# Softplus as one ScalarE function in place of Abs, Relu, Exp, Ln and a VectorE sum

## The chip, the cores and the metric

The kernel runs on one core of a Trainium2 chip. The metric is the device time of one execution in microseconds. A core has TensorE (PE, matmuls and transposes), VectorE (DVE), ScalarE (ACT), GpSimd (POOL) and SyncE (SP, which issues all DMAs here). Each engine runs its own instruction stream in order, and they wait for one another on semaphores.

## The reference

Four sequences of 512 steps pass through a selective state space mixer and a feed-forward part with routed low-rank additions, each followed by a layer norm. D = 2048 channels, N = 16 states, R = 64. Everything is float32.

```python
u, gate = jnp.split(hidden_states @ W_in.T, 2, axis=-1)
u = silu(causal_depthwise_conv(u, conv_w) + conv_b)
dt, Bm, Cm = jnp.split(u @ Wx.T, [R, R + N], axis=-1)      # each then through an rmsnorm
delta = jax.nn.softplus(dt @ Wdt.T + dt_bias)
# per step: state = exp(delta * A) * state + (delta * u) * B ;  y = sum over N of state * C
y = (y + u * D_param) * silu(gate)
x = layernorm(x + y @ W_out.T)
x = layernorm(x + x @ W.T + b + lora(x))
```

## The kernel before

Channels lie on the partitions: D is cut into 16 tiles of 128 channels, time (512) lies along the free axis. The mixer goes through 256 units (b, g, n): sequence b (4), group g of four channel tiles (4), state n (16). A unit is

- on SP a fetch of one row of B for all partitions,
- on POOL `drive` = du times that row (128x2048, L1202),
- on ACT four `decay` = exp(delta * A) (L1038) into three PSUM buffers in turn,
- on DVE four `scan` (L803), which write the states over drive,
- on PE sixteen transposes (`turn`, L674) into two banks `state_t`, which three DVE additions (`add`, L818) and, for the fourth, ACT (`scale`) and POOL (`sum`) weigh with C and add to `y_acc`.

Between the units the engines work off other jobs. Products with W_in and with the feed-forward weights (`u_mm`, `g_mm`, `f_mm`, L698 to L700) run as three passes of a high and a low part. W_out's product (`o_mm`, L721) uses plain float32. `w_high` on ACT (L1072) and `w_low` on POOL (L1228) split weights into these parts. `u_conv`, `u_silu`, `g_tanh` (L1087) and `g_silu` finish the products. At the end of a group `y_turn` on PE turns y back, `y_skip` on DVE (L879) adds D_param * u, and `y_gate` on POOL (L1224) multiplies with the gate. An `o_mm` of sequences 0 to 2 needs all 16 `y_gate` of its sequence. These products share three PSUM banks (`BANKS`), each held from its first matmul until its last reader.

delta is made by `delta_job` for half a group, two tiles, at a time, 32 halves in all. `delta_mm` on PE (L743, L744) makes a tile in a bank. `d_abs` is two ACT passes over it: Abs of x + dt_bias into `delta` (L1119), and Relu of the same back into the bank (L1120). `d_exp` makes exp(-|x|) in `delta` (L1125), `d_ln` makes ln(1 + that) (L1131). `d_sum` on DVE (L848) adds the bank to `delta`, which gives softplus, and gives the bank back. Then `du` on POOL (L1217) makes delta * u for the whole group, ahead of the group's drives, and the decays read delta. The delta of a group is made while the group before it is scanned. That of group 0 is made at the end of the sequence before, or, for sequence 0, before anything is scanned.

The order of every engine's instructions is not written by hand. `make_plan` puts down each piece with a due time and an assumed duration, what it needs and which bank or buffer it takes, and `arrange` walks through time and gives each engine the ready piece with the earliest due time. The instructions are then issued in that order, with waits on the semaphores of what they need. Exp and Ln lie in different function tables here, so that a table load (ACT_TABLE_LOAD), which the compiler places, stands between them.

## Time and profile before

| | |
|---|---|
| median of 3 runs | 2586.82 us (2584.71 to 2592.55) |
| the profiled execution | 2587.63 us, span 2585.8 us |
| TensorE busy | 2216.7 us, 86% |
| VectorE busy | 2191.0 us, 85% |
| GpSimd busy | 1797.8 us, 70% |
| ScalarE busy | 1426.0 us, 55% |
| mean clock granted to TensorE | 0.914 of full speed |

The span runs from the first instruction to the last. Busy time is the time in which an engine executes something, and an engine that is busy for most of the span can still not be the one that others wait for in a given stretch. The trace also says of each instruction how long its engine stood idle before it and which instruction ended that idle time.

### The profile page before, as it was taken

The page shows a single profiled execution, that of the slowest core. Times are in us where ns is not written, and L with a number is a line of the kernel's source. Part 1 is how long each engine was busy: PE and PEld are TensorE (multiplying, and loading weights), DVE is VectorE, ACT ScalarE, POOL GpSimd, SP SyncE. Part 2 cuts the span into 40 slices and gives each one's busy share as a digit, 9 for nine tenths or more (in the row PEclk, how much of TensorE's full clock was granted, in tenths as well). Part 3 has the DMA queues.
Part 4 walks back from the last instruction along what each step waited for, and adds up shares of the span by engine and source line. Part 5 has one row for each costly group of instructions (what it writes and reads, how often), then busy time and mean ns, then how long its engine had stood idle before and what let it go on. Part 6 is the DMA issues. An engine that isn't in the chain of part 4 may idle for free.

```text
span 2585.8 us, 30936 instructions
## 1 busy us (share of the span) xinstructions
PE 2216.7 (86%) x10528; PEld 1609.6 (62%) x10528; DVE 2191.0 (85%) x2681; ACT 1426.0 (55%) x2155; POOL 1797.8 (70%) x768
## 2 busy tenths in 40 slices
PE   6978779887789979899979979899979987888977
PEld 5756557676645557677855556677845556665545
DVE  3449889999969799899969989999978999999831
ACT  3357566664456475655556565655556566554421
POOL 3359989988667679767657866867658887678600
PEclk9988879999879989899979989999969998988988
DMA  4256555554222325755533324556523334343213
GB/s 157 62 187 220 187 184 181 179 188 159 83 76 84 98 90 185 255 179 188 168 101 91 107 86 128 182 191 191 162 79 97 107 92 139 108 162 96 78 49 114
DMA packets 152652, 353.53 MB, mean 137 GB/s; under 512 B 17776, under 2 KB 27376, under 8 KB 152496
## 3 DMA queue, kind: packets, MB, share of 16 engines
q1 hardware_dynamic: 152496, 351.56, 42.4%
q8 instruction: 84, 1.38, 0.2%
q14 instruction: 72, 0.59, 0.1%
HBM read 282.65 MB, written 68.85 MB: 136 GB/s over the span
## 4 chain that ended last, share of the span: by engine, by line
PE 53%; DVE 31%; issue 8%; ACT 4%; POOL 3%; DMA 1%; SPq 0%; DVEq 0%; POOLq 0%; ACTq 0%
PE bank L721 16%; DVE drive L803 14%; PE state_t L674 12%; DVE y_acc L818 7%; PE bank L698 6%; PE bank L700 6%; PE bank L699 6%; PE bank L674 3%; DVE scratch L825 2%; PE bank L756 2%; POOL drive L1202 1%; DVE ln_stats L898 1%; DVE channels L839 1%; PE bank L744 1%; DVE channels L879 1%
## 5 line engine op out<-in xcount | busy, mean ns | idle before, releaser
L1202 POOL TENSOR_TENSOR drive<-delta_u,b_bcast 128x2048 f32<-128x2048 f32 x256 | 1170.9, 4577 | 302.0 <-PE state_t L674 301.0
L803 DVE TENSOR_TENSOR_SCAN drive<-decay,drive 128x512 f32<-128x512 f32 x1024 | 1195.1, 1203 | 34.5 <-POOL drive L1202 30.9
L1038 ACT ACTIVATE decay<-delta,a_sb 128x512 f32<-128x512 f32 x1024 | 700.2, 689 | 474.6 <-DVE drive L803 468.3
L674 PE MATMUL state_t<-identity,drive 128*128 128x128 f32 x4096 | 630.9, 296 | 219.8 <-DVE drive L803 147.5
L674 PEld LDWEIGHTS state_t<-identity,drive 128*128 128x128 f32 x4096 | 510.5, 151 | 433.0 <-DVE drive L803 201.0
L698 PE MATMUL bank<-cols_high,w_split 128*128 128x512 f32 (+1 forms) x1312 | 564.7, 430 | 51.2 <-POOL w_split L1228 37.4
L818 DVE SCALAR_TENSOR_TENSOR y_acc<-state_t,c_rows,y_acc 128x512 f32<-128x512 f32 x720 | 513.8, 735 | 65.0 <-PE state_t L674 60.0
L700 PE MATMUL bank<-cols_high,w_split 128*128 128x512 f32 (+1 forms) x1312 | 528.6, 403 | 0.0
L699 PE MATMUL bank<-cols_low,w_split 128*128 128x512 f32 (+1 forms) x1312 | 527.1, 402 | 0.0
L721 PE MATMUL bank<-channels,w_raw 128*128 128x512 f32 x1024 | 487.3, 607 | 5.9 <-POOL channels L1224 5.3
L1208 POOL TENSOR_TENSOR y_acc<-y_acc,scaled 128x512 f32<-128x512 f32 x240 | 308.9, 1287 | 143.3 <-ACT scaled L1052 143.1
L698 PEld LDWEIGHTS bank<-cols_high,w_split 128*128 128x128 f32 (+1 forms) x1312 | 255.9, 195 | 104.5 <-issue 35.8
L700 PEld LDWEIGHTS bank<-cols_high,w_split 128*128 128x128 f32 (+1 forms) x1312 | 253.8, 193 | 59.8
L721 PEld LDWEIGHTS bank<-channels,w_raw 128*128 128x128 f32 x1024 | 183.2, 195 | 160.8 <-issue 159.7
L699 PEld LDWEIGHTS bank<-cols_low,w_split 128*128 128x128 f32 (+1 forms) x1312 | 256.0, 195 | 42.0
L1052 ACT ACTIVATE scaled<-state_t,c_rows 128x512 f32<-128x512 f32 x240 | 163.6, 682 | 184.5 <-PE state_t L674 150.5
L1228 POOL TENSOR_TENSOR w_split<-w_raw,w_split 128x512 fp32r<-128x512 f32 (+1 forms) x114 | 145.4, 1287 | 121.6 <-ACT w_split L1072 121.6
L825 DVE SCALAR_TENSOR_TENSOR scratch<-bank,conv_w_sb,scratch 128x511 f32<-128x511 f32 (+2 forms) x192 | 142.7, 743 | 46.7 <-ACT scratch L1078 42.2
L1224 POOL TENSOR_TENSOR channels<-channels,scratch 128x512 f32<-128x512 f32 x64 | 80.9, 1277 | 72.5 <-DVE channels L879 72.1
L889 DVE TENSOR_TENSOR rows<-bank,rows 128x512 f32<-128x512 f32 x80 | 54.2, 678 | 90.6 <-PE bank L674 90.2
L1072 ACT ACTIVATE w_split<-w_raw 128x512 fp32r<-128x512 f32 (+1 forms) x114 | 70.4, 620 | 41.6 <-PE bank L700 32.6
L1217 POOL TENSOR_TENSOR delta_u<-delta,channels 128x512 f32<-128x512 f32 x64 | 80.1, 1287 | 14.2 <-DVE delta L848 14.2
(100 smaller groups left out, 1474.6 us busy)
## 6 DMA issues: line engine op xcount, KB each, us to landing
w_split<-w_split SPq DMA_DIRECT2D x288, 512.0 KB, 3.6
b_bcast<-b_rows SPq DMA_DIRECT2D x256, 256.0 KB, 3.4
w_raw<-in_w_out SPq DMA_DIRECT2D x128, 256.0 KB, 2.9
w_raw<-in_w_in SPq DMA_DIRECT2D x96, 256.0 KB, 3.6
gates<-scratch SPq DMA_DIRECT2D x64, 256.0 KB, 2.5
scratch<-gates SPq DMA_DIRECT2D x64, 256.0 KB, 4.7
w_raw<-in_x_cols SPq DMA_DIRECT2D x32, 256.0 KB, 4.1
rows<-in_x_rows SPq DMA_DIRECT2D x4, 2048.0 KB, 9.2
```

Source lines behind the costliest of these rows:

```text
L674: last = engine.transpose(bank[0:tile.shape[1], i * P:(i + 1) * P], tile, identity[:, :])
L698: engine.matmul(bank[:, :], high[:, k % WK, :], cols_high[:, k, :], start=first, stop=False)
L699: engine.matmul(bank[:, :], high[:, k % WK, :], cols_low[:, k, :], start=False, stop=False)
L700: engine.matmul(bank[:, :], low[:, k % WK, :], cols_high[:, k, :], start=False, stop=last).then_inc(signal[stage])
L721: engine.matmul(bank[:, :], tile[:, k % WK, :], chan[s % 2][:, k, :], start=(k == tiles[0]), stop=(k == tiles[-1])).then_inc(signal["o_mm"])
L803: engine.tensor_tensor_scan(state, decay[(GT * s + t) % DECAYS][:, :], state, 0.0, ALU.mult, ALU.add).then_inc(signal["scan"])
L818: engine.scalar_tensor_tensor(y_acc[:, tt, :], bank[:, :], c, y_acc[:, tt, :], ALU.mult, ALU.add).then_inc(signal["add"])
L825: m = engine.scalar_tensor_tensor(conv[:, back:T], bank[:, 0:T - back], conv_w[:, j, KC - 1 - back:KC - back], conv[:, back:T], ALU.mult, ...
L1038: engine.activation(decay[i % DECAYS][:, :], delta[:, g % 2, t, :], ACT.Exp, scale=a_sb[:, j, n:n + 1]).then_inc(signal["decay"])
L1052: engine.activation(scaled[:, :] if n else y_acc[:, ADDED, :], bank[:, :], ACT.Copy, scale=c_rows[b % 2][:, ADDED, n:n + 1]).then_inc(sign ...
L1202: engine.tensor_tensor(drive[key % DRIVES][:, :, :], du[:, :, :], row, ALU.mult).then_inc(signal["drive"])
L1208: engine.tensor_tensor(total, total, scaled[:, :], ALU.add).then_inc(signal["sum"])
```

## The change

`d_abs`, `d_exp`, `d_ln` and `d_sum` become one piece `softplus` on ACT. For the two tiles of a half it runs ACT.Softplus with dt_bias as bias from the bank straight into `delta`, and gives both banks back. The plan assumes 3.8 us for a half. `du` and `decay` now wait for `softplus`. Softplus is in a function table of its own. Apart from that the planner's rules are the same, but since pieces and durations differ, it arrives at another order on all engines.

```diff
--- before.py
+++ after.py
@@ -251,11 +251,8 @@
             key = (b, g, t)
             put("PE", due, 0.46, "delta_mm", key, [there, ("dt_low", b), *old, *beside, *[("delta_mm", (b, g, t - 1))] * (t % 2)],
                 take=[("bank", ("delta_mm", (b, g, x))) for x in tiles] if t % 2 == 0 else [], give=[("dt", w)] if t % 2 else [])
-            put("ACT", due + 0.6, 1.18, "d_abs", key, [("delta_mm", key), *old])
-        put("ACT", due + 0.9, 1.1, "d_exp", (b, g, half), [("d_abs", (b, g, t)) for t in tiles])
-        put("ACT", due + 0.9, 3.7, "d_ln", (b, g, half), [("d_exp", (b, g, half))])
-        for t in tiles:
-            put("DVE", due + 1.2, 0.6, "d_sum", (b, g, t), [("d_ln", (b, g, half))], give=[("bank", ("delta_mm", (b, g, t)))])
+        put("ACT", due + 0.9, 3.8, "softplus", (b, g, half), [("delta_mm", (b, g, t)) for t in tiles] + old,
+            give=[("bank", ("delta_mm", (b, g, t))) for t in tiles])
 
     def y_job(b, g, t, due):
         key, last = (b, g, t), UNITS.index((b, g, N - 1))
@@ -392,7 +389,7 @@
         q = 4 * s
         put("SP", q - 10, 0.35, "fetch", s, [("b_store", b)] + ([("drive", s - 2)] if s > 1 else []), kb=256)
         if n == 0:
-            put("POOL", q - 8.5, 4.95, "du", (b, g), [("d_sum", (b, g, t)) for t in range(GT)] +
+            put("POOL", q - 8.5, 4.95, "du", (b, g), [("softplus", (b, g, half)) for half in range(2)] +
                 [("u_silu", (b, g * GT + t)) for t in range(GT)] + ([("drive", s - 1)] if s else []))
             for half in range(2 if g else 0):
                 delta_job(b, g, half, q - 4 * N + 16 * half + 8)
@@ -402,7 +399,7 @@
             [("turn", (s - DRIVES, tt)) for tt in range(TT)] if s >= DRIVES else [("lora_rest", 0)]))
         for t in range(GT):
             i = GT * s + t
-            put("ACT", i - DECAYS - 0.5, 0.605, "decay", (s, t), [("d_sum", (b, g, t))] + (
+            put("ACT", i - DECAYS - 0.5, 0.605, "decay", (s, t), [("softplus", (b, g, t // 2))] + (
                 [("scan", divmod(i - DECAYS, GT))] if i >= DECAYS else []))
             put("DVE", i, 1.13, "scan", (s, t), [("drive", s), ("decay", (s, t))])
         for tt in range(TT):
@@ -841,11 +838,6 @@
                     bank, gate = banks[place["bank", ("g_mm", key)]], scratch[place["scratch", ("g", key)]]
                     e.wait_ge(*done("g_tanh", key))
                     engine.scalar_tensor_tensor(gate[:, :], gate[:, :], 1.0, bank[:, :], ALU.add, ALU.mult).then_inc(signal["g_silu"])
-                elif stage == "d_sum":
-                    b, g, t = key
-                    dst = delta[:, g % 2, t, :]
-                    e.wait_ge(*done("d_ln", (b, g, t // 2)))
-                    engine.tensor_tensor(dst, banks[place["bank", ("delta_mm", key)]][:, :], dst, ALU.add).then_inc(signal["d_sum"])
                 elif stage == "dt_low":
                     e.wait_ge(*done("dt_cols", key))
                     if key:
@@ -1032,7 +1024,7 @@
                     s, t = key
                     b, g, n = UNITS[s]
                     j, i = g * GT + t, GT * s + t
-                    e.wait_ge(*done("d_sum", (b, g, t)))
+                    e.wait_ge(*done("softplus", (b, g, t // 2)))
                     if i >= DECAYS:
                         e.wait_ge(*done("scan", divmod(i - DECAYS, GT)))
                     engine.activation(decay[i % DECAYS][:, :], delta[:, g % 2, t, :], ACT.Exp, scale=a_sb[:, j, n:n + 1]).then_inc(signal["decay"])
@@ -1108,28 +1100,18 @@
                     e.wait_ge(*done("ssm_turn_b", key))
                     engine.activation(cols[0:N, :], banks[place["bank", ("ssm_turn_b", key)]][0:N, :], ACT.Copy,
                                       scale=b_ln_w[:, :]).then_inc(signal["b_cols"])
-                elif stage == "d_abs":
-                    b, g, t = key
-                    j, bank = g * GT + t, banks[place["bank", ("delta_mm", key)]]
-                    e.wait_ge(*done("delta_mm", key))
-                    if (b, g) >= (0, 2):
-                        b0, g0 = (b, g - 2) if g >= 2 else (b - 1, g + 2)
-                        e.wait_ge(*done("decay", (UNITS.index((b0, g0, N - 1)), t)))
-                        e.wait_ge(*done("du", (b0, g0)))
-                    engine.activation(delta[:, g % 2, t, :], bank[:, :], ACT.Abs, bias=dt_bias[:, j:j + 1])
-                    engine.activation(bank[:, :], bank[:, :], ACT.Relu, bias=dt_bias[:, j:j + 1]).then_inc(signal["d_abs"])
-                elif stage == "d_exp":
+                elif stage == "softplus":
                     b, g, half = key
                     for t in (2 * half, 2 * half + 1):
-                        e.wait_ge(*done("d_abs", (b, g, t)))
-                        m = engine.activation(delta[:, g % 2, t, :], delta[:, g % 2, t, :], ACT.Exp, scale=-1.0)
-                    m.then_inc(signal["d_exp"])
-                elif stage == "d_ln":
-                    b, g, half = key
-                    e.wait_ge(*done("d_exp", key))
-                    for t in (2 * half, 2 * half + 1):
-                        m = engine.activation(delta[:, g % 2, t, :], delta[:, g % 2, t, :], ACT.Ln, bias=1.0)
-                    m.then_inc(signal["d_ln"])
+                        j = g * GT + t
+                        e.wait_ge(*done("delta_mm", (b, g, t)))
+                        if (b, g) >= (0, 2):
+                            b0, g0 = (b, g - 2) if g >= 2 else (b - 1, g + 2)
+                            e.wait_ge(*done("decay", (UNITS.index((b0, g0, N - 1)), t)))
+                            e.wait_ge(*done("du", (b0, g0)))
+                        m = engine.activation(delta[:, g % 2, t, :], banks[place["bank", ("delta_mm", (b, g, t))]][:, :], ACT.Softplus,
+                                              bias=dt_bias[:, j:j + 1])
+                    m.then_inc(signal["softplus"])
                 elif stage in ("o_copy", "f_copy"):
                     s, h = key[:2]
                     cols = scratch_of((stage[0], key))
@@ -1212,7 +1194,7 @@
                         e.wait_ge(*done("drive", UNITS.index((b, g, 0)) - 1))
                     for t in range(GT):
                         j = g * GT + t
-                        e.wait_ge(*done("d_sum", (b, g, t)))
+                        e.wait_ge(*done("softplus", (b, g, t // 2)))
                         e.wait_ge(*done("u_silu", (b, j)))
                         m = engine.tensor_tensor(du[:, t, :], delta[:, g % 2, t, :], chan[b % 2][:, j, :], ALU.mult)
                     m.then_inc(signal["du"])
```

Lines of the changed kernel lie lower: its softplus is L1112, decay L1030, g_tanh L1079, w_high L1064, scan L800, drive L1184, w_low L1210, du L1199, y_gate L1206, turns L671, o_mm L718, delta_mm L740 and L741, products L695 to L697.

Three places of the order follow. The first is on ScalarE at the program's start, where the second half of group 0's delta is made; before, from the `w_high` of dt_slot on:

```order
L1072 ACTIVATE dt_slot<-w_raw 128x256
L1119 ACTIVATE delta<-bank,dt_bias_sb 128x512
L1120 ACTIVATE bank<-bank,dt_bias_sb 128x512
L1087 ACT_TABLE_LOAD
L1087 ACTIVATE scratch<-bank 128x512
L1125 ACTIVATE delta<-delta 128x512 x2
L1072 ACTIVATE w_split<-w_raw 128x512
L1131 ACT_TABLE_LOAD
L1131 ACTIVATE delta<-delta 128x512 x2
L1072 ACTIVATE w_split<-w_raw 128x512 x2
L1038 ACT_TABLE_LOAD
L1038 ACTIVATE decay<-delta,a_sb 128x512
```

and in the changed kernel, from the same instruction on:

```order
L1064 ACTIVATE dt_slot<-w_raw 128x256
L1112 ACT_TABLE_LOAD
L1112 ACTIVATE delta<-bank,dt_bias_sb 128x512 x2
L1079 ACT_TABLE_LOAD
L1079 ACTIVATE scratch<-bank 128x512
L1064 ACTIVATE w_split<-w_raw 128x512
L1030 ACTIVATE decay<-delta,a_sb 128x512
L1112 ACT_TABLE_LOAD
L1112 ACTIVATE delta<-bank,dt_bias_sb 128x512 x2
L1064 ACTIVATE w_split<-w_raw 128x512
L1030 ACT_TABLE_LOAD
```

The Abs and Relu passes around it are gone, and one load, two Softplus passes and one load stand where Exp, load, Ln and load stood. Before, the second half's passes begin only behind the last row shown; in the changed kernel its Softplus is the second L1112 pair, in the same rows.

The second is on GpSimd at the start of sequence 1. The four L1208 are the last additions to y_acc of sequence 0, L1224 is y_gate, L1217 du, L1202 drive. Before:

```order
L1208 TENSOR_TENSOR y_acc<-y_acc,scaled 128x512
L1202 TENSOR_TENSOR drive<-delta_u,b_bcast 128x2048
L1208 TENSOR_TENSOR y_acc<-y_acc,scaled 128x512 x4
L1224 TENSOR_TENSOR channels<-channels,scratch 128x512 x4
L1217 TENSOR_TENSOR delta_u<-delta,channels 128x512 x4
L1202 TENSOR_TENSOR drive<-delta_u,b_bcast 128x2048 x5
L1208 TENSOR_TENSOR y_acc<-y_acc,scaled 128x512
```

and in the changed kernel, where these are L1190, L1206, L1199 and L1184:

```order
L1190 TENSOR_TENSOR y_acc<-y_acc,scaled 128x512
L1184 TENSOR_TENSOR drive<-delta_u,b_bcast 128x2048
L1190 TENSOR_TENSOR y_acc<-y_acc,scaled 128x512 x4
L1206 TENSOR_TENSOR channels<-channels,scratch 128x512 x2
L1199 TENSOR_TENSOR delta_u<-delta,channels 128x512 x4
L1206 TENSOR_TENSOR channels<-channels,scratch 128x512
L1184 TENSOR_TENSOR drive<-delta_u,b_bcast 128x2048 x4
L1206 TENSOR_TENSOR channels<-channels,scratch 128x512
```

du has moved ahead of the last two y_gate, and the last y_gate behind four drives. At the starts of sequences 2 and 3 the last one stands behind two drives.

The third is on TensorE at the same place. Before, behind the first half's delta_mm, with the last turns of sequence 0, y_turn (from y_acc), the second half's delta_mm and then W_out's product:

```order
L674 MATMUL state_t<-identity,drive 128x128 x8
L674 MATMUL bank<-identity,y_acc 128x128 x16
L743 MATMUL bank<-dt_cols,dt_slot 128x512
L744 MATMUL bank<-cols_rest,dt_slot 128x512
L743 MATMUL bank<-dt_cols,dt_slot 128x512
L744 MATMUL bank<-cols_rest,dt_slot 128x512
L721 MATMUL bank<-channels,w_raw 128x512 x18
L674 MATMUL state_t<-identity,drive 128x128 x8
```

and in the changed kernel:

```order
L671 MATMUL state_t<-identity,drive 128x128 x8
L740 MATMUL bank<-dt_cols,dt_slot 128x512
L741 MATMUL bank<-cols_rest,dt_slot 128x512
L740 MATMUL bank<-dt_cols,dt_slot 128x512
L741 MATMUL bank<-cols_rest,dt_slot 128x512
L671 MATMUL bank<-identity,y_acc 128x128 x16
L695 MATMUL bank<-cols_high,w_split 128x512
L696 MATMUL bank<-cols_low,w_split 128x512
L697 MATMUL bank<-cols_high,w_split 128x512
```

Both halves' delta_mm now stand ahead of y_turn. Behind y_turn stand 48 matmuls of products (the last three rows, sixteen times over) where 18 of W_out's stood, and W_out's product begins behind these, another pair of delta_mm and 28 transposes of the new sequence's units.

## Rows read from the trace of the kernel before

**Rows 1.** The page: busy time, the chain by engine, and one group of matmuls.

```profile
PE 2216.7 (86%) x10528; PEld 1609.6 (62%) x10528; DVE 2191.0 (85%) x2681; ACT 1426.0 (55%) x2155; POOL 1797.8 (70%) x768
...
PE 53%; DVE 31%; issue 8%; ACT 4%; POOL 3%; DMA 1%; SPq 0%; DVEq 0%; POOLq 0%; ACTq 0%
...
L698 PE MATMUL bank<-cols_high,w_split 128*128 128x512 f32 (+1 forms) x1312 | 564.7, 430 | 51.2 <-POOL w_split L1228 37.4
```

**Rows 2.** Busy by stretches, two sums and one stretch; columns PE, PEld, DVE, ACT, POOL.

```profile
sum 1465.00, PE 1242.65 PEld 976.40 DVE 1400.07 ACT 842.26 POOL 1095.28; mean PE 310.66 PEld 244.10 DVE 350.02 ACT 210.56 POOL 273.82
...
sum 393.00, PE 383.50 PEld 215.26 DVE 371.66 ACT 234.94 POOL 315.20; mean PE 127.83 PEld 71.75 DVE 123.89 ACT 78.31 POOL 105.07
...
177.00:325.00 148.00, 117.83 (x577) 91.71 (x576) 131.80 (x144) 96.06 (x154) 142.51 (x67) 0.87 0.62 208
```

**Rows 3.** The same two sets of stretches, d_sum (L848) alone.

```profile
sum 1465.00, DVE 17.77; mean DVE 4.44
...
sum 393.00, DVE 7.62; mean DVE 2.54
```

**Rows 4.** ScalarE's groups of instructions by line: count, busy us, mean ns, idle before.

```profile
L1038 ACT ACTIVATE decay<-delta,a_sb 128x512 f32<-128x512 f32 x1024 | 700.2, 689 | 474.6 <-DVE drive L803 468.3 <-DVE delta L848 3.5
...
L1072 ACT ACTIVATE w_split<-w_raw 128x512 fp32r<-128x512 f32 (+1 forms) x114 | 70.4, 620 | 41.6 <-PE bank L700 32.6 <-issue 4.6 <-DMA w_raw<-in_w_in 4.0
L1078 ACT ACTIVATE scratch<-bank,conv_b_sb,conv_w_sb 128x512 f32<-128x512 f32 x64 | 49.5, 775 | 41.4 <-PE bank L700 41.2
...
L1119 ACT ACTIVATE delta<-bank,dt_bias_sb 128x512 f32<-128x512 f32 x64 | 43.8, 685 | 30.7 <-PE bank L744 30.7
L1120 ACT ACTIVATE bank<-bank,dt_bias_sb 128x512 f32<-128x512 f32 x64 | 42.0, 657 | 0.0
L1131 ACT ACT_TABLE_LOAD x32 | 41.1, 1283 | 0.6
...
L1087 ACT ACTIVATE scratch<-bank 128x512 f32<-128x512 f32 x64 | 37.9, 592 | 36.5 <-PE bank L700 35.9
...
L1125 ACT ACTIVATE delta<-delta 128x512 f32<-128x512 f32 x64 | 36.8, 632 | 0.0
L1131 ACT ACTIVATE delta<-delta 128x512 f32<-128x512 f32 x64 | 36.8, 622 | 0.4
```

**Rows 5.** VectorE's groups of instructions by line.

```profile
L803 DVE TENSOR_TENSOR_SCAN drive<-decay,drive 128x512 f32<-128x512 f32 x1024 | 1195.1, 1203 | 34.5 <-POOL drive L1202 30.9 <-ACT decay L1038 3.1
...
L848 DVE TENSOR_TENSOR delta<-bank,delta 128x512 f32<-128x512 f32 x64 | 40.7, 676 | 32.0 <-ACT delta L1131 32.0
```

**Rows 6.** Timelines at the program's start: start us, us, engine, line, [idle before].

```profile
151.57 0.41 ACT L1072 ACTIVATE dt_slot<-w_raw 128x256 fp32r<-128x256 f32 x1
...
168.57 1.29 DVE L848 TENSOR_TENSOR delta<-bank,delta 128x512 f32<-128x512 f32 x2 [8.21 <-ACT delta L1131]
...
169.34 2.55 POOL L1217 TENSOR_TENSOR delta_u<-delta,channels 128x512 f32<-128x512 f32 x2 [4.72 <-DVE delta L848]
...
171.84 1.31 POOL L1228 TENSOR_TENSOR w_split<-w_raw,w_split 128x512 fp32r<-128x512 f32 x1
...
173.08 4.64 POOL L1202 TENSOR_TENSOR drive<-delta_u,b_bcast 128x2048 f32<-128x2048 f32 x1
...
177.75 1.22 DVE L803 TENSOR_TENSOR_SCAN drive<-decay,drive 128x512 f32<-128x512 f32 x1 [5.45 <-POOL drive L1202]
```

**Rows 7.** Timelines at the start of sequence 1, from three engines.

```profile
738.03 0.75 DVE L879 SCALAR_TENSOR_TENSOR channels<-channels,d_param_sb,bank 128x512 f32<-128x512 f32 x1 [1.21 <-PE bank L674]
...
738.92 1.29 POOL L1224 TENSOR_TENSOR channels<-channels,scratch 128x512 f32<-128x512 f32 x1 [0.69 <-DVE channels L879]
...
743.63 17.20 PE L721 MATMUL bank<-channels,w_raw 128*128 128x512 f32 x36 [0.23 <-POOL channels L1224]
...
748.23 1.29 DVE L848 TENSOR_TENSOR delta<-bank,delta 128x512 f32<-128x512 f32 x2 [6.64 <-ACT delta L1131]
...
756.16 4.57 DVE L803 TENSOR_TENSOR_SCAN drive<-decay,drive 128x512 f32<-128x512 f32 x4 [6.65 <-POOL drive L1202]
```


## Prediction

> **What bounds the kernel now.** I read the page first. Its busy line has TensorE at 86%, VectorE at 85%, GpSimd at 70% and ScalarE at 55%, and the chain that ended last is 53% TensorE, 31% VectorE and only 4% ScalarE [rows 1]. The reader should see two engines that share the bound, and that the four passes sit on the engine with most room. ScalarE time is therefore worth nothing by itself; it counts where somebody waits for delta.
>
> Next I took busy time by stretches, because the bound moves. Four stretches (400 to 725, 890 to 1325, 1490 to 1915, 2070 to 2350 us, together 1465 us) have VectorE busy for 1400 us, 96%, and TensorE for 1243 us, 85% [rows 2]: VectorE sets the pace. Three stretches in which W_out's matmuls run (756 to 890, 1356 to 1490, 1945 to 2070, together 393 us) have TensorE at 384 us, 98%, and VectorE at 372 us, 95% [rows 2]: TensorE sets the pace, with VectorE right behind. From 177 to 325 us GpSimd is busy for 143 of 148 us [rows 2]. Between these lie the program's start, before the first scan at 177.75 us [rows 6], and the starts of sequences 1, 2 and 3, where VectorE's trace has real holes. All three look alike; in the first VectorE is idle 6.64 us before the d_sum of the second half and 6.65 us before the next scan [rows 7].
>
> Last I read the groups of instructions of ScalarE and VectorE for the cost of each pass [rows 4, 5].
>
> **What goes and what comes.** There are 64 delta tiles. ScalarE loses Abs (43.8 us), Relu (42.0), Exp (36.8) and Ln (36.8), 159.4 us in all [rows 4]. It gains 64 Softplus passes, which no row shows. The nearest row is Abs, with the same shape, the same PSUM source and the same bias operand: 685 ns. The bounds are a pass from PSUM with no operand per partition, 592 ns, and one with two, 775 ns [rows 4]. I take 685 ns, 43.8 us together; the bounds make 37.9 and 49.6 us. ScalarE's relief is 159.4 - 43.8 = 116 us (110 to 121). I book it at nothing: ScalarE was idle 474.6 us before its decay passes, 468.3 of them until a scan had ended [rows 4], and VectorE's scans waited for a decay only 3.1 us in the whole run [rows 5].
>
> Table loads neither go nor come. Before, a load of 1283 ns stands ahead of each of the 32 pairs of Ln [rows 4], and one ahead of whatever needs the other table next. In the new order one stands ahead of each of the 32 pairs of Softplus and one behind; counting every load of ScalarE's program, both kernels have 87. So the block on ScalarE, load, two passes, load, stays what it was: 1.28 + 1.24 + 1.28 = 3.8 us before, 1.28 + 1.37 + 1.28 = 3.9 us after. Three decay buffers, each good for a scan of 1.2 us, cover 3.6 us of it and the adds between the scans cover the rest; the 3.1 us says so. If that cover were gone, 32 blocks of 0.1 us more would cost 4 us.
>
> Here a rule of the notes speaks against the change. The Trainium skill, page "ScalarE: Activation LUTs", section "Table sets: the hidden batching unit", says that one set holds both exp and ln, so that Exp followed by Ln needs no second load. By that rule the old path could have gone without its loads and the change would add 64, by the rows' 1283 ns 82 us of ScalarE. This trace disagrees for this build: Ln has its 32 loads [rows 4].
>
> VectorE loses 64 d_sum additions, 40.7 us busy [rows 5], and gains nothing. It also stood idle for 32.0 us until Ln had ended [rows 5]. Two of the three banks are held from delta_mm to d_sum before, to Softplus now, so they come back earlier.
>
> **The sum, place by place.**
>
> Program start, -6 us. ScalarE's dt_slot ends at 151.57 + 0.41 = 152.0 us; d_sum of the second half starts at 168.57, du's second pair at 169.34, the first drive at 173.08, the first scan at 177.75 [rows 6]. In the new order a load and two Softplus follow dt_slot: 152.0 + 1.28 + 1.3 = 154.6. The second half's matmuls wait for those banks alone (before, for one that g_silu gave back and one that d_sum did): four matmuls at 0.43 us [rows 1] make 156.3. On ScalarE stand a load, g_tanh, w_high, a decay and a load (1.28 + 0.59 + 0.62 + 0.69 + 1.28 = 4.5 us [rows 4]), from 154.6 to 159.1; then the two Softplus, to 160.4. GpSimd: two du (2.55) to 163.0, three w_low (1.3 each, where one stood before) to 166.8, drive (4.6) to 171.4 [rows 6]. The first scan at 171.5 is 6 us sooner. With one w_low as before it would be 9.
>
> Stretches where VectorE sets the pace, -18 us. They hold 17.8 us of the 40.7 [rows 3]. I take all of it, since VectorE is idle only 4% there.
>
> Stretches of W_out, -2 us. They hold 7.6 us of it [rows 3], but TensorE keeps its 384 us of work; a quarter is what I give for VectorE being so near. The remaining 15.3 us stand before 400 us, where GpSimd leads, and in the holes; they count nothing.
>
> Starts of sequences 1, 2 and 3, -3 us each: -9 us. y_skip of tile 1 starts at 738.03 and its y_gate at 738.92 for 1.29 us [rows 7], so it ends at 740.2. The new order of GpSimd puts du behind two y_gate instead of four, and TensorE computes both halves of delta ahead of y_turn, so du no longer waits: 740.2 + 5.1 (four du) + 1.3 (a third y_gate) + 4.6 (drive) = 751.2 against 756.16 for the scan [rows 7], 5 us sooner. TensorE limits what is left of it. Before, 18 o_mm filled the hole, 17.20 us from 743.63 to 760.8 [rows 7], when the turns of the new unit could begin. Now 48 product matmuls stand there: at 0.43 us 20.6 us, from the end of y_turn near 740.8 to 761.4. The adds behind the turns gain nothing, the scans ahead of them do. Hence 3 of 5, with bounds 0 and 5.
>
> Total -6 - 18 - 2 - 9 = -35 us. The profiled execution took 2587.63 us (its span is 2585.8, with 1.8 around it), so 2552.6; the median of the three runs, 2586.82, lies 0.8 lower, so I say **2552 us**.
>
> **The rivals.**
>
> *All of VectorE's time comes back.* The 40.7 us and, of the 32.0 us of waits for Ln, all but the start's share that is counted there already: about -70, 2517 us. For it speaks that VectorE is busy 95% even in W_out's stretches; against it TensorE's 98% there [rows 2]. Chance 0.15.
>
> *The relief lands beside the path.* Only the start and a little more come through, since TensorE and GpSimd keep their work: -9, 2578 us. For it: 53% of the chain is TensorE's [rows 1]. Against it: VectorE at 96% over 1465 us [rows 2]. Chance 0.13, half of it within 0.3% of no change.
>
> *W_out's matmuls come too late (slower).* At the first of the three starts the new order moves the last y_gate behind four drives (behind two at the others), and every o_mm needs all 16 y_gate. The 17.2 us of o_mm that filled each hole move into a stretch where TensorE has 2% to spare: 3 x 17.2 = 52 us, less 35, so +17, 2603 us. It decides from the point where TensorE idles for more than 35 / 3 = 12 us in each hole. The 48 product matmuls that stand there speak against it, as they come out of the same stretch. Chance 0.07.
>
> *Softplus is no plain pass.* If it took two passes' time (1.37 us), the block on ScalarE would be 5.3 us and exceed the 3.6 us of three scans; 32 x 1.4 = 44 us, half of it beside adds: -35 + 22, 2574 us. Every row of a 128x512 pass lies between 592 and 775 ns [rows 4]. Chance 0.05.
>
> The forecast itself has 0.60, from 2535 to 2568 us.
>
> **Range and chances.** Eight in ten reach from near the first rival to the second: 2520 to 2580 us. A measurement of this kernel tells about 0.3%, 8 us, from no change. Faster by more: forecast 0.60, first rival 0.15, half of the second 0.07, a longer Softplus 0.04, 0.86 together. Within: 0.08. Slower: 0.06.
>
> **What would show it.** No d_sum, and VectorE busy about 41 us less; 64 Softplus near 685 ns and ScalarE near 1310 us busy; 87 loads of 1283 ns; the first scan near 171.5 us; at the three starts no wait before a second half, and the next scan some 13 us behind y_skip of tile 1 instead of 18; VectorE's wait for decay still under 10 us. I'd be wrong if new idle time of VectorE in its own stretches ate the 18 us, if TensorE idled before the first o_mm of a sequence, or if the planner's new order, which differs in small things everywhere, made waits of its own.

## The result, and the profile after

The changed kernel takes 2611.85 us in the median, the kernel before 2586.82 in the same set of runs: a ratio of 1.0096 with a 95% interval from 1.0063 to 1.013, some 25 us slower. The prediction of 2552 us was wrong in sign, and the range did not hold the time. The nearest rival was one to which I had given 0.07, W_out's matmuls that come too late, at +17 us. The differences of times below are differences of medians. The kernel before has medians from 2586.8 to 2590.8 us in the sets of runs, so differences to the changed kernel come out 3 to 8 us larger by the ratios.

The page of the changed kernel, its busy line, and then the groups of ScalarE and VectorE by line that answer to [rows 1, 4, 5]:

```profile
PE 2233.1 (86%) x10528; PEld 1622.3 (62%) x10528; DVE 2160.8 (83%) x2617; ACT 1323.3 (51%) x1962; POOL 1796.1 (69%) x768
```

```profile
L1030 ACT ACT_TABLE_LOAD x40 | 51.3, 1283 | 0.7
L1112 ACT ACTIVATE delta<-bank,dt_bias_sb 128x512 f32<-128x512 f32 x64 | 41.1, 684 | 16.7 <-PE bank L741 16.2
L1112 ACT ACT_TABLE_LOAD x32 | 41.1, 1283 | 0.6
...
L800 DVE TENSOR_TENSOR_SCAN drive<-decay,drive 128x512 f32<-128x512 f32 x1024 | 1195.4, 1206 | 18.5 <-POOL drive L1184 13.9 <-ACT decay L1030 4.2
```

The local effects went the way that was forecast, though not all in full: Softplus (L1112) is a pass of 684 ns, VectorE has 64 instructions and 30 us less to do (41 were forecast), and ScalarE 103 us less (116 were forecast). The scans waited 4.2 us for a decay, 1.1 more than before. TensorE, with the same 10,528 matmul records, is busy 16 us longer.

So I went through the program by units. The table gives the difference in the start of a unit's first scan, the changed kernel minus the kernel before, in us (a sequence has 64 units; the last scan is in unit 255).

| unit | 0 | 12 | 60 | 64 | 80 | 84 | 124 | 144 | 148 | 208 | 212 | 255 |
|---|---|---|---|---|---|---|---|---|---|---|---|---|
| after - before | -4.6 | +12.6 | -3.3 | -8.1 | -11.3 | +9.9 | +7.9 | +3.0 | +18.8 | +13.0 | +32.4 | +23.9 |

Up to unit 80 the change wins, with a detour at the start. Then it loses 21, 16 and 19 us in three jumps, each over the four units in which the W_out matmuls of the sequence before come to their end. The timeline of VectorE at the first jump, and under it TensorE's, each with start, duration and the idle time before in brackets:

```profile
869.77 2.33 DVE L800 TENSOR_TENSOR_SCAN drive<-decay,drive 128x512 f32<-128x512 f32 x2
883.34 0.69 DVE L881 TENSOR_TENSOR rows<-bank,rows 128x512 f32<-128x512 f32 x1 [11.24 <-PE bank L671]
897.51 0.69 DVE L881 TENSOR_TENSOR rows<-bank,rows 128x512 f32<-128x512 f32 x1 [13.48 <-PE bank L671]
907.39 1.41 DVE L871 SCALAR_TENSOR_TENSOR channels<-channels,d_param_sb,bank 128x512 f32<-128x512 f32 x2 [9.19 <-PE bank L671]
```

```profile
869.82 13.04 PE L718 MATMUL bank<-channels,w_raw 128*128 128x512 f32 x30
882.70 0.60 PE L671 MATMUL bank<-identity,scratch 128*128 128x128 f32 x4
883.14 13.90 PE L718 MATMUL bank<-channels,w_raw 128*128 128x512 f32 x32
896.87 0.60 PE L671 MATMUL bank<-identity,scratch 128*128 128x128 f32 x4
897.31 9.61 PE L718 MATMUL bank<-channels,w_raw 128*128 128x512 f32 x22
```

VectorE is out of scans at 872.1 us and stands idle for 11.24 + 13.48 + 9.19 = 33.9 us, since TensorE has 84 records of W_out matmuls, with only eight transposes between them, ahead of the turns that VectorE waits for. (A W_out matmul leaves two records in a trace. Where no records are named, matmuls of W_out are counted by instructions: 128 for each sequence.) The kernel before had 26 and 22 records there, and VectorE was idle for 4.54 + 9.19 us.

Part of it is decided at the other end of the stretch. At the start of the sequence GpSimd's last y_gate now comes behind du and four drives, and no W_out matmul can go without it. GpSimd's and TensorE's timelines at that place:

```profile
742.12 1.30 POOL L1206 TENSOR_TENSOR channels<-channels,scratch 128x512 f32<-128x512 f32 x1
743.37 13.62 POOL L1184 TENSOR_TENSOR drive<-delta_u,b_bcast 128x2048 f32<-128x2048 f32 x3
758.14 4.53 POOL L1184 TENSOR_TENSOR drive<-delta_u,b_bcast 128x2048 f32<-128x2048 f32 x1 [1.15 <-PE state_t L671]
762.61 1.28 POOL L1206 TENSOR_TENSOR channels<-channels,scratch 128x512 f32<-128x512 f32 x1
...
764.14 2.04 PE L718 MATMUL bank<-channels,w_raw 128*128 128x512 f32 x2 [0.64 <-POOL channels L1206]
```

The first W_out matmul starts at 764.14 us instead of 743.63 [rows 7]. In the hole stand 48 product matmuls; they were pulled forward from the units behind number 80. That much follows from two traces; what of it costs the time had to be tried.

### The profile page after: what moved, and what is told of

It reads as the page before. It is cut to its first block and busy times, and to the rows that moved or that the text cites. A ratio compares the mean times of both kernels' runs of the same rounds, so it can differ in the third digit from the quotient of the medians.

```text
span 2610.1 us, 30598 instructions
## 1 busy us (share of the span) xinstructions
PE 2233.1 (86%) x10528; PEld 1622.3 (62%) x10528; DVE 2160.8 (83%) x2617; ACT 1323.3 (51%) x1962; POOL 1796.1 (69%) x768
## 5 line engine op out<-in xcount | busy, mean ns | idle before, releaser
L1184 POOL TENSOR_TENSOR drive<-delta_u,b_bcast 128x2048 f32<-128x2048 f32 x256 | 1170.1, 4575 | 288.9 <-PE state_t L671 288.2
L800 DVE TENSOR_TENSOR_SCAN drive<-decay,drive 128x512 f32<-128x512 f32 x1024 | 1195.4, 1206 | 18.5 <-POOL drive L1184 13.9
L1030 ACT ACTIVATE decay<-delta,a_sb 128x512 f32<-128x512 f32 x1024 | 700.1, 689 | 484.3 <-DVE drive L800 481.2
L671 PE MATMUL state_t<-identity,drive 128*128 128x128 f32 x4096 | 644.4, 300 | 252.5 <-DVE drive L800 182.6
L671 PEld LDWEIGHTS state_t<-identity,drive 128*128 128x128 f32 x4096 | 520.7, 154 | 468.4 <-DVE drive L800 235.8
L695 PE MATMUL bank<-cols_high,w_split 128*128 128x512 f32 (+1 forms) x1312 | 567.2, 432 | 34.9 <-POOL w_split L1210 32.9
L697 PE MATMUL bank<-cols_high,w_split 128*128 128x512 f32 (+1 forms) x1312 | 528.6, 403 | 0.0
L718 PE MATMUL bank<-channels,w_raw 128*128 128x512 f32 x1024 | 481.7, 602 | 5.5 <-POOL channels L1206 5.5
L1190 POOL TENSOR_TENSOR y_acc<-y_acc,scaled 128x512 f32<-128x512 f32 x240 | 308.5, 1286 | 128.2 <-ACT scaled L1044 128.0
L695 PEld LDWEIGHTS bank<-cols_high,w_split 128*128 128x128 f32 (+1 forms) x1312 | 257.0, 196 | 85.5 <-issue 31.3
L697 PEld LDWEIGHTS bank<-cols_high,w_split 128*128 128x128 f32 (+1 forms) x1312 | 254.8, 194 | 60.5
L718 PEld LDWEIGHTS bank<-channels,w_raw 128*128 128x128 f32 x1024 | 181.2, 193 | 157.2 <-issue 156.9
L1210 POOL TENSOR_TENSOR w_split<-w_raw,w_split 128x512 fp32r<-128x512 f32 (+1 forms) x114 | 144.9, 1280 | 172.8 <-ACT w_split L1064 171.7
L881 DVE TENSOR_TENSOR rows<-bank,rows 128x512 f32<-128x512 f32 x80 | 54.4, 681 | 136.6 <-PE bank L671 136.0
L1206 POOL TENSOR_TENSOR channels<-channels,scratch 128x512 f32<-128x512 f32 x64 | 81.1, 1280 | 90.8 <-DVE channels L871 87.1
L1064 ACT ACTIVATE w_split<-w_raw 128x512 fp32r<-128x512 f32 (+1 forms) x114 | 70.3, 620 | 55.8 <-PE bank L697 35.9
L1120 ACT ACTIVATE scratch<-bank 128x512 f32<-128x512 f32 x48 | 28.4, 593 | 102.0 <-PE bank L718 102.0
```

Of the source, the lines that this page charges most:

```text
L671: last = engine.transpose(bank[0:tile.shape[1], i * P:(i + 1) * P], tile, identity[:, :])
L695: engine.matmul(bank[:, :], high[:, k % WK, :], cols_high[:, k, :], start=first, stop=False)
L697: engine.matmul(bank[:, :], low[:, k % WK, :], cols_high[:, k, :], start=False, stop=last).then_inc(signal[stage])
L718: engine.matmul(bank[:, :], tile[:, k % WK, :], chan[s % 2][:, k, :], start=(k == tiles[0]), stop=(k == tiles[-1])).then_inc(signal["o_mm"])
L800: engine.tensor_tensor_scan(state, decay[(GT * s + t) % DECAYS][:, :], state, 0.0, ALU.mult, ALU.add).then_inc(signal["scan"])
L1030: engine.activation(decay[i % DECAYS][:, :], delta[:, g % 2, t, :], ACT.Exp, scale=a_sb[:, j, n:n + 1]).then_inc(signal["decay"])
```

## The experiments

The ratios are to the kernel before, run on the same chip. "Products" are the matmuls of g for the coming sequence.

### The new instructions in the old order

The plan keeps the pieces and costs of before, so all other instructions stand in the order of before; the pieces of Abs, Exp and the sum emit nothing, and the one of Ln emits two Softplus.

```diff
-                    m = engine.activation(delta[...], delta[...], ACT.Ln, bias=1.0)
+                    m = engine.activation(delta[...], banks[place["bank", ("delta_mm", (b, g, t))]][:, :], ACT.Softplus, bias=...)
...
-                    engine.tensor_tensor(dst, banks[...][:, :], dst, ALU.add).then_inc(signal["d_sum"])
```

> Softplus in one pass and no sum on VectorE, with the order of all other instructions on TensorE, GpSimd and SyncE as in the kernel before. Theory A, that the changed order loses the time (the matmuls of W_out leave the hole at the start of a sequence and lengthen the stretch behind it, three jumps of 16 to 21 us in the trace of after): without the order the savings stay, so 2550 to 2575 us, faster than before by 12 to 36 us, and no jump of more than 5 us between units 80 and 84, 144 and 148, 208 and 212. Theory B, that the new instruction or its waits cost the time (one pass of 684 ns holds a bank for VectorE in another way, decay comes late): the time is lost in this order too, 2600 us or more. Theory C, that the savings lie beside the path and the rest is noise of the order: within 8 us of the kernel before.

Measured: 2564.87 us, ratio 0.9901 [0.9878, 0.9924]. Theory A holds, and B and C fall: the one pass makes the kernel 26 us faster, and only the order that came with it makes it slower. Its difference to before is -18.8 us at unit 80 and -19.9 at unit 84; there is no jump. VectorE's timeline where the W_out matmuls end has 4.55 + 9.19 us of idle time instead of 33.9:

```profile
861.09 3.42 DVE L805 TENSOR_TENSOR_SCAN drive<-decay,drive 128x512 f32<-128x512 f32 x3
869.06 0.69 DVE L889 TENSOR_TENSOR rows<-bank,rows 128x512 f32<-128x512 f32 x1 [4.55 <-PE bank L676]
878.95 1.41 DVE L879 SCALAR_TENSOR_TENSOR channels<-channels,d_param_sb,bank 128x512 f32<-128x512 f32 x2 [9.19 <-PE bank L676]
```

### VectorE's part and ScalarE's part alone

Both in the order of before. The first drops VectorE's sums but keeps four passes on ScalarE, the last of them Softplus; the second makes one pass and keeps 64 passes on VectorE, as a maximum in place of the sum, so that its delta is not softplus. Of the edits only the second pass of the first kernel is shown:

```diff
-                    engine.activation(bank[:, :], bank[:, :], ACT.Relu, bias=...)
+                    engine.activation(bank[:, :], bank[:, :], ACT.Identity)
```

> VectorE's part alone: its 64 sums are gone, ScalarE still makes four passes for each delta (the last of them the Softplus, the second an Identity in place of Relu, in place on the bank), all in the order of the kernel before. Theory A: VectorE's relief is most of the saving, so the time is 5 to 30 us under the kernel before and within 10 us of the run with one pass in the same order. Theory C, the relief lies beside the path: within 8 us of the kernel before. Theory B expects it 10 us or more above the kernel before, since the Softplus itself is in it.

> ScalarE's part alone: one Softplus pass for each delta, while VectorE keeps its 64 passes from the bank (as a maximum, so that the work is the same and the value is not), all in the order of the kernel before. Theory A: ScalarE is idle half of the span, so this gives only the shorter start and the shorter waits for delta, 0 to 12 us under the kernel before (2575 to 2587). Theory B expects it 10 us or more above the kernel before. If ScalarE's passes were what the groups wait for, it gives nearly all that the run with one pass and no sum gives.

Measured: 2578.01 us, 0.9954 [0.9929, 0.9979], and 2581.28 us, 0.9965 [0.9946, 0.9984]. Each part is worth something, by the ratios 12 and 9 us, and their sum of 21 is near the 26 of both. The first missed one of its bounds: it is 13 us above the run with both, not within 10. I had booked ScalarE's passes at nothing but the start. The trace of the second has its first scan 3.7 us sooner and its last 7.6, so half of its gain lies behind the start.

### du behind the four y_gate

The changed kernel with one need more for GpSimd's du of the first group.

```diff
                 [("u_silu", (b, g * GT + t)) for t in range(GT)] + ([("drive", s - 1)] if s else [])
+                + ([("y_gate", (b - 1, NG - 1, t)) for t in range(GT)] if b and g == 0 else [])
```

> The changed kernel with one thing moved: at the start of sequences 1 to 3 GpSimd's du of the first group is planned behind all four y_gate, so that 16 of the W_out matmuls of the last group come into the hole again and 18 to 24 products instead of 48 to 72. Theory A: a part of the three jumps of 16 to 21 us goes with the matmuls that go (112 instead of 128 stand behind the hole), but the first drive comes 6 to 8 us later at each start: 2585 to 2605 us, 7 to 27 us under the changed kernel. Theory B and C: the time stays at that of the changed kernel or rises by the later drive, 2610 to 2635 us.

Measured: 2590.3 us, ratio 0.9993 [0.9978, 1.0009], by the medians 21 us under the changed kernel. The three jumps shrink: unit 84 minus unit 80 is 55.4 us, against 69.3 in the changed kernel and 48.1 in the kernel before. As expected.

### The products behind the last W_out matmul

The changed kernel, its products at the starts forbidden ahead of the end of W_out; no W_out matmul comes back into the hole.

```diff
     def split_product(stage, key, tile, due, needs, scratch):
+        if stage == "g_mm" and 0 < key[0] and key[1] >= max(GATES_BEFORE[key[0]], 8):
+            needs = [*needs, ("o_mm", (key[0] - 1, HT - 1, DT - 1))]
```

> The changed kernel with one thing moved: the later products of g and delta at the start of sequences 1 to 3 are planned behind the last matmul of W_out, so that the hole holds none of them, while all 128 matmuls of W_out still stand behind the hole. It tells apart what of the order costs: if the late W_out matmuls are the cost (theory A as it stands), nothing comes back, 2605 to 2620 us, and the hole is merely empty. If what counts is how the products stand among the W_out matmuls of the stretch, 2585 to 2600 us.

Measured: 2591.79 us, ratio 0.9988 [0.9968, 1.0008]. My theory as it stood, that the late W_out matmuls are the whole loss, falls here: all of them still stand behind the hole, unit 84 minus unit 80 is as much (70.0 us), and yet some 20 us come back, because each of the three starts is shorter. What a late W_out costs by itself is told by the run with both moves, further down.

### Late W_out in the kernel before

The kernel before, its W_out planned behind the fourth drive of the next sequence.

```diff
-                [("y_gate", (s, j // GT, j % GT)) for j in tiles]),
+                [("y_gate", (s, j // GT, j % GT)) for j in tiles] + ([("drive", PER_SEQ * (s + 1) + 3)] if s + 1 < NSEQ else [])),
```

> The kernel before, with its four passes and its sums, and one thing moved: no W_out matmul may stand ahead of the fourth drive of the next sequence, which gives TensorE nearly the order that the changed kernel has at the three starts (48 to 78 products in the hole, 128 W_out matmuls behind it). Theory A: the three jumps come without Softplus, 30 to 60 us over the kernel before, 2617 to 2650 us. Theory B and C: within 10 us of the kernel before.

Measured: 2674.63 us, ratio 1.0314 [1.0284, 1.0344], 84 us or so above the kernel before. The three jumps come without Softplus, so B and C fall once more, but the size is beyond the bounds. Between units 60 and 84 it has the 48 products and 128 W_out matmuls of the changed kernel and takes 244.0 us where that one takes 229.7. Counts alone don't set the time. (The execution that left the trace took 2685.97 us, 11 more than the median.) Over the six stretches that the next section defines, it takes 709.4 us and the changed kernel 667.7. Of these 42 us more, 28 are idle time of TensorE (94 against 66), and of those, 18 are transposes that wait for a scan (66 against 48). Why the scans are later there, this run does not tell.

### Both moves together

The two diffs above in one kernel.

> The changed kernel with both moves at once: du of the first group planned behind the four y_gate, and the later products planned behind the last matmul of W_out. The hole at the start of sequences 1 to 3 then holds 17 W_out matmuls and no product, as in the kernel before (18 and 0, 30, 0). If the two things that each gave about 20 us are two parts of one loss of about 45 us (the pile of W_out matmuls behind the last turn of the stretch, and the products in the hole), this comes to the time of the one pass in the order of before: 2558 to 2575 us. If each move alone already gave all that there is to give, it stays at 2585 to 2595 us.

Measured: 2572.06 us, ratio 0.9917 [0.9888, 0.9947]: the two moves add up, to 40 of the 47 us that lie between the changed kernel and the one pass in the old order. Its interval overlaps that of the one pass in the old order, so the 7 us that are left are not shown to be a difference.

This run and the one with the products moved differ by the need of du alone, and through it by 17 W_out matmuls in each hole against none. That is worth 20 us of the time, with a first drive that comes later in it. It shows where VectorE waits for W_out's result to be turned back into rows. The row of that wait, with its total, its count and its longest, first with the products moved, then with both moved:

```profile
DVE rows L884 <- PE bank L674: 141.9, 28, 13.5
```

```profile
DVE rows L885 <- PE bank L675: 86.0, 23, 11.4
```

It is 136.0 us in the changed kernel and 89.5 in the one pass in the old order. So a late W_out does cost time by itself.

The view by stretches shows what the loss is made of. I cut each trace at the first scans of units 60, 64 and 84, 124, 128 and 148, and 188, 192 and 212, which gives the three starts and the three W_out stretches. The sums, first of the changed kernel, then of the one pass in the old order, of the run with the products moved, and of the run with both moves:

```profile
sum 667.70, PE 601.95 PEld 363.24 DVE 523.73 ACT 315.05 POOL 463.02; mean PE 100.32 PEld 60.54 DVE 87.29 ACT 52.51 POOL 77.17
```

```profile
sum 622.50, PE 560.48 PEld 328.29 DVE 514.90 ACT 309.55 POOL 456.79; mean PE 93.41 PEld 54.72 DVE 85.82 ACT 51.59 POOL 76.13
```

```profile
sum 623.30, PE 552.15 PEld 327.11 DVE 515.94 ACT 299.40 POOL 458.62; mean PE 92.02 PEld 54.52 DVE 85.99 ACT 49.90 POOL 76.44
```

```profile
sum 609.10, PE 545.82 PEld 322.26 DVE 515.44 ACT 302.17 POOL 458.31; mean PE 90.97 PEld 53.71 DVE 85.91 ACT 50.36 POOL 76.39
```

TensorE's idle time in them is nearly the same in all four (65.8, 62.0, 71.2 and 63.3 us), so between these four the length goes mostly with TensorE's busy time. Counted by their start, 224 product matmuls lie in these stretches of the changed kernel, and 65, 32 and 32 in the others. (By TensorE's order, from the first turn of unit 60 to the first of unit 84 and so on, there are 192, 72, 69 and 69.) TensorE spends 59.2 us on the 224 and 16.6 on the 65; this difference of 42.6 is as large as the 41.5 us of TensorE's time that the changed kernel has more than the one pass in the old order. The length is 45.2 us more.

Two things keep this from being the whole account. The 45.2 us are 17.5, 12.8 and 15.0 at the three starts, while TensorE's order has 18, 30 and 72 products more there. And the two last runs hold the same number of products, yet the one with a late W_out takes 14.2 us more (623.3 against 609.1).

The products were taken from the stretches right behind (from the first scan of unit 84 to that of unit 96, and so on: units 84 to 96, 148 to 160, 212 to 224). By TensorE's order these hold 450 products in the changed kernel and 576 in the old order. These are the sums of the changed kernel and of the one pass in the old order:

```profile
sum 308.00, PE 237.77 PEld 179.52 DVE 291.93 ACT 188.19 POOL 241.04; mean PE 79.26 PEld 59.84 DVE 97.31 ACT 62.73 POOL 80.35
```

```profile
sum 318.80, PE 262.72 PEld 202.00 DVE 303.46 ACT 192.43 POOL 246.69; mean PE 87.57 PEld 67.33 DVE 101.15 ACT 64.14 POOL 82.23
```

VectorE is busy for 95% there, and 25 us less of TensorE's work shorten them by 10.8 us only. Work moved from where it was partly free to where it counts more: 45.2 - 10.8 = 34 of the 53 us between the last scans of the two traces. Of the rest, 12.5 us arise in sequence 0, before unit 60, and 6 elsewhere; I have located these and not explained them. Such a loss before unit 60 is there in each run whose order is planned with the one pass: against the one pass in the old order it is 16.5 us with du moved, 16.6 with the products moved, 21.2 with both moved, and 32.9 in the run of the next section. (The trace of the old order is of an execution 6 us under its median, so 53 us stand in the traces where the medians give 47.)

### One number of the plan

The changed kernel with a pair of Softplus planned at the 1.4 us that it takes, instead of 3.8.

```diff
-        put("ACT", due + 0.9, 3.8, "softplus", ...
+        put("ACT", due + 0.9, 1.4, "softplus", ...
```

> The changed kernel, with one number of the planner changed: a pair of Softplus is planned at 1.4 us, the time that the trace shows for two of them (2 x 684 ns), instead of 3.8 us. Not an instruction is changed. The order then has 30, 78 and 57 products and 16, 11 and 10 W_out matmuls in the three holes, and 64, 45 and 42 instead of 74, 57 and 53 W_out matmuls in the last four turns of the stretch. If the order alone sets the loss, 10 to 25 us come back, 2585 to 2602 us; if the order of after is only one of many equal ones, 2605 to 2617 us.

Measured: 2594.88 us, ratio 1.0009 [0.9992, 1.0027], within what the order was expected to give: no instruction differs, and 17 us come back. Its six stretches hold as many products as the changed kernel's (224 by their start), and 37 W_out matmuls in the holes instead of none:

```profile
sum 632.80, PE 580.56 PEld 351.75 DVE 520.53 ACT 316.02 POOL 462.25; mean PE 96.76 PEld 58.62 DVE 86.76 ACT 52.67 POOL 77.04
```

TensorE is idle for 52 us here, not 66, and about as many matmuls (2,410 against 2,395 records) take 21 us less, at the clock told below. So these stretches are only 10.3 us longer than those of the one pass in the old order (632.8 against 622.5), with the same 159 products more that go with 45.2 us in the changed kernel. The number of products in a stretch doesn't price an order: how TensorE's waits and its clock fall between them weighs as much. Of the 35 us between the last scans of the two traces, 33 arise before unit 60; the stretches behind W_out and later give 8 back.

### The old passes in the new order

The changed kernel's order on every engine, with the four passes in Softplus's place and the sums put into VectorE's order where the plan has a pair of Softplus done.

```diff
+    late = [(now + 3.93, "d_sum", (b, g, 2 * half + t)) for (_, (b, g, half)), now in at.items() for t in range(2)]
+    plan.work["DVE"] = sorted(plan.work["DVE"] + late, key=lambda piece: piece[0])
```

> The fourth corner: the four passes and the sum of the kernel before, in the order that the changed kernel has on every engine. If order and instructions add up, it stands to the changed kernel as the kernel before stands to the one pass in the old order, 20 to 32 us above it (2630 to 2645 us), so the order alone costs 40 to 55 us whichever form softplus has. If the order is bad only together with the one pass, it comes to 2590 to 2615 us.

Measured: 2716.01 us, ratio 1.0481 [1.0459, 1.0504]. Neither expectation holds; it is 104 us above the changed kernel where the same instructions cost 26 in the old order. The groups of VectorE have the reason for a part of it, the sum (L853):

```profile
L853 DVE TENSOR_TENSOR delta<-bank,delta 128x512 f32<-128x512 f32 x64 | 41.2, 686 | 62.1 <-ACT delta L1134 62.0
```

VectorE stands 62 us at its sums, 30 more than in the kernel before [rows 5], presumably since they are placed for a plan in which ScalarE's block ends sooner than eight passes do. So this corner doesn't measure the order alone.

### The old order with both moves

> The one pass in the order of the kernel before, and in it the products of the starts planned behind the last matmul of W_out and du behind the four y_gate, so that the holes hold 17 W_out matmuls and no product in all three starts (18 with 0, 30 and 0 products before). The trace of the run that moved both in the changed kernel had 205, 213 and 203 us or so from the fourth-last unit of a sequence to the twentieth behind it, 4 to 7 us less than the one pass in the old order at the first start, but it had lost 21 us by unit 60, in the order of the first sequence, which the old order does not lose. If these two parts are independent, this is the fastest of all: 2548 to 2562 us, 3 to 15 us under the one pass in the old order. If the order of sequence 0 and that of the starts hang together, or if the start gains are given back later, it comes to 2562 to 2575 us.

Measured: 2575.78 us, ratio 0.9952 [0.9934, 0.9969], the second case, and above even that. The diffs are the two from above, put on the one pass in the old order. Its six stretches sum to 623.1 us, not the 609.1 of the run that has the same moves in the changed kernel, although both have 17 W_out matmuls and no product in each hole. Against the one pass in the old order it loses 5 us before unit 60, 9 right behind the W_out stretches and 7 behind unit 224, and gains 4 between. What makes these differences stays open. The same two moves take 40 us off the changed kernel and add 11 us here, so neither has a price of its own that holds in any order.

## Why the prediction was wrong

**The step that failed** is the sentence in the slower rival that the 48 product matmuls "speak against it, as they come out of the same stretch". By TensorE's order that holds for 30 of the 48 at the first start and for 42 of 72 at the second, and for none of the 72 at the third; the other 120 came out of the next stretches, where VectorE sets the pace. From that sentence came both the chance of 0.07 and the missing term: the sum prices the planner's new order at nothing. The runs put +47 us in its place (2611.85 against 2564.87 us for the same instructions in the old order), of which du and W_out moved back take off 21, the products moved back 20, and both 40. Had I counted, per stretch, the matmuls that TensorE gets and loses, the order would have shown 120 more in stretches where TensorE was already busy 90%. At the 0.26 us that the changed kernel's trace has for each (59.2 us for 224) that is an estimate of 31 us, and a warning about the sign. It would not have been a forecast: nearly the same count belongs to the order planned at 1.4 us, whose stretches are only 10.3 us longer.

**The rival's own mechanism** was half right. It said that TensorE would idle in the hole and pay the 17.2 us of W_out matmuls later, and that this decides from 12 us of idle time. The hole does not idle more: TensorE was idle for 13.9 us between units 60 and 64, and 16.8 in the kernel before. Its work stands there, but other work. That W_out is paid for later is right: with the products fixed, the late W_out makes the six stretches 14.2 us longer (623.3 against 609.1 us), not 3 x 17.2. Its +17 us came out near the +25 in part by luck, as the moved products are in it nowhere.

**The start**, -6: measured -4.6 us in the first scan (-5.0 in the old order). The first scan came at 173.2 us, not 171.5: GpSimd's du ended at 163.5 (163.0 in the sum), and it then stood idle for 1.3 us until the weight of the third w_low was there, which the sum has not. Softplus at 685 ns: 684. The 87 table loads: 40 + 32 + 8 + 4 + 1 + 1 + 1 = 87 in the groups by line. VectorE's wait for a decay under 10 us: 4.2.

**Stretches where VectorE sets the pace**, -18: hidden by the order in the changed kernel. In the old order 10.7 us come between units 0 and 60, 1.6 in the stretches right behind W_out and 4.3 in the rest, 16.7 in all. So the size is near, but the place isn't: most of it lies in sequence 0.

**The starts, -9, and W_out, -2**: in the old order the three starts are 10.9 us shorter and the W_out stretches 3.2 us longer, 7.7 together. In the changed kernel the first scan of a sequence does come sooner, 13.0 us behind y_skip of tile 1 (735.05 to 748.02 us), as forecast, and it is worth 4.8 us at the first start; at unit 84 the 4.8 and 13.2 more are gone. The sum had the hole's products at 0.43 us each, 20.6 us, up to 761.4; they were done near 750, since TensorE's granted clock rose from 1.2 to 2.4 GHz at 740.4 and they start 0.23 us apart from there. In this order the gain at the head of the stretch did not last to its end.

So the terms of the sum that concern the instructions, -35 us, measured -25.6 by the ratio when nothing else moved. The term that was missing, the order, measured +47 (2611.85 against 2564.87 us): by the traces 34 of 53 us at the three starts, the W_out stretches and the stretches right behind them.

**Is the rest a cause or noise?** Seven of these kernels with the one pass, each in its own order, lie between 2565 and 2612 us. That spread is as wide as any gain at stake. It isn't noise: the intervals of the changed kernel and of the one pass in the old order lie 1.4% apart. The fastest by its median, the one pass in the old order, is the version that I would keep: 26 us under the kernel before, 47 under the changed one.

## What to carry to other kernels

Where a planner sets the order, a faster instruction is two changes: the instruction, and a new order. Measure the first with the order held still. For the second, count each engine's work by stretch, before and after: work that enters a stretch can count in full where that engine is the bound there, and what leaves another stretch gives back only what that stretch's own bound allows. Such a count warns of the sign; here it did not give the size, as two orders with the same count were 35 us apart in these stretches. So don't book a new order at nothing: give it a term with wide bounds, or build it once both ways. An engine with a full hole isn't a good sign by itself; ask which later stretch the work in it was meant to relieve.

## What the runs showed of the hardware

TensorE's granted clock in the holes differs from order to order. The windows of the first start, in the changed kernel and in the run planned at 1.4 us (the number behind the engines' busy times is the clock as a share of 2.4 GHz):

```profile
695.50:748.00 52.50, 38.60 (x144) 28.48 (x145) 33.41 (x39) 23.15 (x31) 31.72 (x18) 0.61 0.17 55
```

```profile
716.00:768.30 52.30, 39.83 (x152) 27.76 (x153) 33.59 (x39) 23.17 (x31) 32.73 (x19) 0.80 0.19 60
```

The mean of 0.61 is made of time at 1.2 and at 2.4 GHz. It is 0.61 in the one pass in the old order too, whose hole holds W_out matmuls and no product, so it isn't set by the kind of matmul alone. The first start's W_out stretch, right behind, was at 0.94 in the one and at 0.97 in the other, at 0.99 in the one pass in the old order and at 1.00 with both moves.

So a part of what I count as TensorE's busy time is clock. By the clock in the traces TensorE was busy at 1.2 GHz for 107 us of the six stretches in the changed kernel, for 88 in the one pass in the old order, and for 56 in the run planned at 1.4 us. In the first hole of the changed kernel the product matmuls start 0.43 us apart while the granted clock is 0.50 (to 740.4 us), and 0.23 apart at 1.00. If all of that busy time would take half as long at 2.4 GHz, the lower clock costs 53, 44 and 28 us of busy time; this is an estimate. By it the changed kernel's 41.5 us more than the old order are some 9 us of clock and 32 of work, and the 21 us that the order planned at 1.4 us gains on it, with about the same matmuls, are clock.
